# One DMA transpose over 2048 columns in place of two over 1024 in both attentions of a four-layer block

## The chip, the cores and the metric

The kernel runs on one core of a Trainium2 chip. The metric is the device time in microseconds (us) of one execution.
The engines are named as in the profile: PE is TensorE's matmul, PEld its weight load, DVE VectorE, ACT ScalarE, POOL GpSimd, SP SyncE, which here only issues DMAs (SPq is its queue).

## The reference

Four sublayers in turn act on x of 4 batches of 512 tokens by 256 features. Each takes the layernorm of x and adds its result to x:

1. a cross-attention with 16 heads of 64 over 508 keys of a context of 4 x 512 x 192, with low-rank updates of its weights and a second small attention over the last 4 context rows ("A" in the kernel's names);
2. a mixture of 8 experts ("M");
3. a cross-attention with 8 heads of 64 over 512 keys ("C");
4. a gated feed-forward layer with rounded activations and weights ("F").

The attentions are what matters here. For each batch and head:

```
s = jnp.einsum('bhid,bhjd->bhij', q, k) * SCALE
p = jax.nn.softmax(s, axis=-1)
o = jnp.einsum('bhij,bhjd->bhid', p, v)
```

The sum over keys j in the third line needs p with j on the partitions, so p, which is made with queries i on the partitions, has to be transposed.

## The kernel before

One function, `attention`, emits both attentions, C without the low-rank and 4-row parts. Work is cut into G steps. A step n is one block of 128 queries for one pair of heads: 4 batches x 8 pairs x 4 query blocks = 128 steps in A and 4 x 4 x 4 = 64 in C. Half h of a pair is numbered e = 2n + h. A step goes through five engines:

- PE `scores(n)` (L603): six matmuls into two PSUM banks, one for each head; the pair of banks is shared by every second step.
- DVE (L949): one reduction finds both heads' row maxima.
- ACT `weights(n)`: for each head, the exponential twice, once rounded to fp16 into the ring `PHL` (L752, the high part, 8 slots) and once in fp32 into the ring `pr` (L753, 3 slots).
- POOL (L465): for each head, the low part = fp32 minus high part, into the second half of the same slot of `PHL`. It raises `pl_ready` once per head.
- SP (L412): for each head, a DMA transpose of the slot (128 partitions by 1024 columns of fp16: 512 high, 512 low, 256 KB) into half h of `PT[n % 4]`. It waits for `pl_ready` of that head, and on the first head for `pv_done` of step n-4, which frees the buffer.
- PE `weigh(n)` (L621 to L623): 24 matmuls with the transposed blocks as weights. It waits until both transposes of the step have landed (`pt_loaded[n % 4]`).

Each engine's order is written out by hand. PE runs, for g = 0, 1, ...: `scores(g)`, then the jobs that a table plans for g (projections of q and k, transposes of x and of the output, the output projection), then `weigh(g - 3)` (`LAG = 3`). ACT runs `weights(g - 1)` and then copies out the jobs of g. So `scores(n + 4)` stands right behind `weigh(n)` on PE. On SP some plain DMAs stand between the transposes: in A eight loads of the value matrices for the next batch (`load_v`), in both the load of the next batch's context `CT`. `weights(n)` also waits for the transposes of step n-4, which frees its slots of `PHL`.

Of the kernel before, what the change touches and what calls it, by code (L numbers as in the profile page):

```python
# [68 lines left out]
def turn_of(stats, group, nc, name, total):  # L69

    made = stats["turns"].setdefault(group, {})
    if name not in made:
        made[name] = [stats["scope"].enter_context(nc.semaphore(f"{group}_{name}")), 0]
    turn = Turn(made[name][0], made[name][1])
    made[name][1] += total
    return turn
# [58 lines left out]
def attention(nc, tag, X, ident, identb, stats, w, ctx_t, heads, ipa, scratch, x_in=None):  # L135
# [6 lines left out]
    G = B * U  # L142
    KEYS = N - IPA if ipa else N
    HIPA = heads * IPA
    LAG, RING, PRING, PTS, SLOTS, VBANKS = 3, 3, 8, 4, 2, 4
# [37 lines left out]
    with ctx:  # L183
        def sb(name, shape, dt, within=ctx):
            return within.enter_context(nc.sbuf_tensor(f"{tag}_{name}", shape, dt))

        def sem(name, total):
            return turn_of(stats, "attn", nc, name, total)
# [4 lines left out]
        def wait(eng, s, n):  # L193
            eng.wait_ge(s.sem, s.base + n)
# [13 lines left out]
        PHL = sb("PHL", [P, PRING, 2, N], F16)  # L208
        PT = [sb(f"PT{k}", [P, 2, 2 * QT, P], F16) for k in range(PTS)]
# [84 lines left out]
        ws_hi = ipa_sem("ws_hi")  # L294
        ws_split = ipa_sem("ws_split")

        pt_loaded = [sem(f"pt_loaded{k}", 32 * G // PTS) for k in range(PTS)]
        xn_ready = sem("xn_ready", B)
        bias_added = sem("bias_added", B)
        pj_filled = sem("pj_filled", len(jobs))  # L300
# [5 lines left out]
        pl_ready = sem("pl_ready", 2 * G)  # L306
# [18 lines left out]
        def _(sp):  # L325
# [23 lines left out]
            def load_v(b, kt):  # L349
                wait(sp, v_stored[kt], 32 * (B - 1))  # L350
                sp.dma_start(VH[b % 2][:, kt, :, :].rearrange("p h d -> p (h d)"), scratch["vh"][b][:, kt]).then_inc(v_loaded[b % 2].sem, 16)
                sp.dma_start(VL[b % 2][:, kt, :, :].rearrange("p h d -> p (h d)"), scratch["vl"][b][:, kt]).then_inc(v_loaded[b % 2].sem, 16)
# [52 lines left out]
            for n in range(G):  # L405
                b, u = n // U, n % U
                if n >= PTS:
                    wait(sp, pv_done, n - PTS + 1)
                for h in range(2):
                    e = 2 * n + h  # L410
                    wait(sp, pl_ready, e + 1)
                    sp.dma_start_transpose(out=PT[n % PTS][:, h, :, :],  # L412
                                           in_=PHL[:, e % PRING, :, :].rearrange("p s n -> p (s n)")).then_inc(pt_loaded[n % PTS].sem, 16)
                if b + 1 < B:
                    if ipa and 6 <= u < 6 + QT:
                        load_v(b + 1, u - 6)
                    if u == U - 7:
                        if ipa and b == 0:
                            wait(sp, ct_stored[0], 32)
                        wait(sp, pj_filled, JOB["k", b, PAIRS - 1] + 1)  # L420
                        sp.dma_start(CT[:, :, :].bitcast(F32), scratch["ct"][b + 1]).then_inc(ct_loaded[0].sem, 16)
# [53 lines left out]
        def _(pe):  # L475
# [130 lines left out]

            def weigh(n):
                b, c = n // U, n // QT % PAIRS
                wait(pe, pt_loaded[n % PTS], 32 * (n // PTS + 1))
                if n % 2 == 0 and n >= 4:  # L610
                    wait(pe, o_ready, n // 2 - 1)
                if ipa and b and n % U == 0:
                    wait(pe, v_loaded[b % 2], 128 * ((b + 1) // 2))
                vh, vl = VH[b % VBUFS], VL[b % VBUFS]
                for h in range(2):
                    m = (2 * (n % 2) + h) * (DH + 1)
                    o = ps[:, O_BANK + n // 2 % 2, m:m + DH + 1]
                    for kt in range(QT):
                        r = slice(0, P - (N - KEYS) if kt == QT - 1 else P)
                        hi, lo = PT[n % PTS][r, h, kt, :], PT[n % PTS][r, h, QT + kt, :]  # L620
                        mm(o, hi, vh[r, kt, 2 * c + h, :], start=(kt == 0 and h == 0 and n % 2 == 0), stop=False)  # L621
                        mm(o[:, 0:DH], hi, vl[r, kt, 2 * c + h, :], start=False, stop=False)  # L622
                        last = mm(o, lo, vh[r, kt, 2 * c + h, :], start=False, stop=(kt == QT - 1 and h == 1 and n % 2 == 1))  # L623
                last.then_inc(pv_done.sem, 1)
# [51 lines left out]
            for g in range(G + TAIL):  # L676
                if g < G:
                    scores(g)
                for kind, b, k in at.get(g, []):
                    if (kind, b, k) == ("o", 0, 0):  # L680
                        wait(pe, w_split, 4)
                    RUN[kind](b, k)
                if LAG <= g < G + LAG:
                    weigh(g - LAG)

        @block.scalar
        def _(a):
# [55 lines left out]
            def weights(n):  # L743
                wait(a, max_ready, n + 1)
                if n >= PTS:
                    wait(a, pt_loaded[n % PTS], 32 * (n // PTS))
                for h in range(2):
                    e = 2 * n + h
                    o = ps[:, S_BANK + 2 * (n % 2) + h, 0:KEYS]
                    if e >= RING:  # L750
                        wait(a, pl_ready, e - RING + 1)
                    a.activation(PHL[:, e % PRING, 0, 0:KEYS], o, ACT.Exp, bias=nm[:, n % 4, h:h + 1])  # L752
                    a.activation(pr[:, e % RING, 0:KEYS], o, ACT.Exp, bias=nm[:, n % 4, h:h + 1]).then_inc(p_ready.sem, 1)  # L753
# [48 lines left out]
            for g in range(G + TAIL):  # L802
                if 1 <= g <= G:
                    weights(g - 1)
                for u in at.get(g, []):
                    if u[0] in HI_KINDS:
                        high(u)
                if ipa and g < G and g % U == 17:
                    wait(a, ipa_sub, g // U + 1)
                    a.activation(SI[:, 0:QT * heads, :], SI[:, 0:QT * heads, :], ACT.Exp).then_inc(ipa_exp.sem, 1)  # L810
# [957 lines left out]
def network(nc, a, out):  # L1768
    with ExitStack() as ctx:
# [32 lines left out]
        def spare(name, shape, dt):  # L1802
# [6 lines left out]
        }  # L1809
        ctx_t = chunks(a["ctxT"], P)  # L1810
        attention(nc, "A", X, ident, identb, stats, {
            "q": chunks(a["L0_xattn_Wq"], P), "k": chunks(a["wk0"], P), "v": chunks(a["wv0"], P),
            "o": chunks(a["L0_xattn_Wo"], P), "bias": a["bo"], "alpha": a["alpha"], "down": a["down"],
# [6 lines left out]
            "w_out": a["L0_ffn_w_out"].rearrange("e (c p) n -> e p c n", p=P),  # L1820
        })
        attention(nc, "C", X, ident, identb, stats, {
            "q": chunks(a["L1_xattn_Wq"], P), "k": chunks(a["wk1"], P), "v": chunks(a["wv1"], P),
            "o": chunks(a["L1_xattn_Wout"], P), "bias": a["bout"],
# [45 lines left out]
```

## Time and profile before

| | |
|---|---|
| median of 3 runs | 1273.2 us (1271.38 to 1277.29) |
| the profiled execution | 1267.05 us, span 1265.3 us |
| busy share of the span | PE 75%, PEld 58%, DVE 57%, ACT 60%, POOL 52% |
| first attention, steps | about 142 to 592 us of the span |
| third sublayer's attention, steps | about 904 to 1133 us of the span |

The profile is of one execution. Busy shares are over the whole span, with stages of different limits. PE's ends are modelled, since its matmuls are pipelined, so a busy PE isn't PE at its peak. Instructions that issue DMAs do not count as busy, but the trace has their durations. "To landing" counts from the start of an issue to the last update of its semaphore.

### The profile page before, as it was taken

Reading aid. Unit: us, or ns where it says so; the run is one execution under the profiler, and the core shown is the slowest. Engines: PE = TensorE matmul, PEld = TensorE weight load, DVE = VectorE, ACT = ScalarE, POOL = GpSimd, SP = SyncE. Lnnn points to the kernel's source line nnn. Section 1 sums busy time; section 2 is a strip of 40 time slices with the busy share of each in tenths; the row PEclk is TensorE's granted clock in tenths of the full one; section 3 lists DMA queues with packets and bytes.
Section 4 is the critical chain, followed back from the end, with each engine's and each line's share of the span. In section 5 each row is a group of like instructions: output and inputs, shape, how many; then the busy total and the mean of one; then the engine's idle time right before and its main releaser. Section 6 shows DMA issues by size and latency. Waiting matters only on the chain. (4 is left out here: it accounts for less than half of the span.)

```text
span 1265.3 us, 24199 instructions
## 1 busy us (share of the span) xinstructions
PE 954.9 (75%) x9167; PEld 735.3 (58%) x9174; DVE 725.7 (57%) x1301; ACT 757.2 (60%) x1265; POOL 655.7 (52%) x564
## 2 busy tenths in 40 slices
PE   2578778999989999997441999933788888862675
PEld 2456656767666676776330899932556666652343
DVE  3742256765866676573547344437465666538776
ACT  3331387887977788794242444402597787754576
POOL 2420176676776667673257555413186676653121
PEclk9787599999999999997655999976998999976799
DMA  9740299999899899896253222235299998972001
GB/s 251 262 170 5 46 201 166 178 188 198 157 181 203 151 180 171 138 166 111 69 181 98 71 77 77 65 114 190 58 174 172 165 175 151 151 126 100 5 26 39
DMA packets 444193, 171.01 MB, mean 135 GB/s; under 512 B 410128, under 2 KB 427728, under 8 KB 444048
## 3 DMA queue, kind: packets, MB, share of 16 engines
q1 hardware_dynamic: 440336, 159.23, 62.8%
q0 software_dynamic: 3744, 10.23, 2.6%
q8 instruction: 76, 1.25, 0.4%
q14 instruction: 37, 0.30, 0.1%
HBM read 49.68 MB, written 19.05 MB: 54 GB/s over the span
## 5 line engine op out<-in xcount | busy, mean ns | idle before, releaser
L465 POOL TENSOR_TENSOR A_PHL<-A_pr,A_PHL 128x508 f16<-128x508 f32 x256 | 295.2, 1157 | 157.5 <-ACT A_pr L753 157.2
L949 DVE TENSOR_REDUCE A_negmax<-A_ps 128x2 f32<-128x1016 f32 x128 | 155.4, 1214 | 74.3 <-PE A_ps L603 73.7
L465 POOL TENSOR_TENSOR C_PHL<-C_pr,C_PHL 128x512 f16<-128x512 f32 x128 | 148.1, 1163 | 86.5 <-ACT C_pr L753 85.9
L752 ACT ACTIVATE A_PHL<-A_ps,A_negmax 128x508 f16<-128x508 f32 x256 | 179.0, 699 | 21.5 <-DVE A_negmax L949 21.0
L753 ACT ACTIVATE A_pr<-A_ps,A_negmax 128x508 f32<-128x508 f32 x256 | 180.7, 706 | 0.0
L621 PE MATMUL A_ps<-A_VH,A_PT 128*128 128x65 bf16 (+1 forms) x1024 | 110.1, 197 | 34.3 <-DMA A_PT<-A_PHL 33.7
L603 PE MATMUL A_ps<-A_K,A_Q 64*128 64x508 f32 x768 | 125.9, 433 | 11.0 <-ACT A_pr L753 8.9
L621 PEld LDWEIGHTS A_ps<-A_VH,A_PT 128*128 128x128 f16 (+1 forms) x1024 | 93.8, 98 | 64.6 <-DMA A_PT<-A_PHL 52.2
L622 PE MATMUL A_ps<-A_VL,A_PT 128*128 128x64 f16 (+1 forms) x1024 | 109.2, 194 | 0.0
L623 PE MATMUL A_ps<-A_VH,A_PT 128*128 128x65 bf16 (+1 forms) x1024 | 108.9, 195 | 0.0
L949 DVE TENSOR_REDUCE C_negmax<-C_ps 128x2 f32<-128x1024 f32 x64 | 78.2, 1222 | 43.7 <-PE C_ps L603 43.5
L623 PEld LDWEIGHTS A_ps<-A_VH,A_PT 128*128 128x128 f16 (+1 forms) x1024 | 95.8, 98 | 0.0
L622 PEld LDWEIGHTS A_ps<-A_VL,A_PT 128*128 128x128 f16 (+1 forms) x1024 | 95.7, 100 | 0.2
L752 ACT ACTIVATE C_PHL<-C_ps,C_negmax 128x512 f16<-128x512 f32 x128 | 90.3, 706 | 5.1 <-DVE C_negmax L949 4.7
L753 ACT ACTIVATE C_pr<-C_ps,C_negmax 128x512 f32<-128x512 f32 x128 | 91.2, 712 | 0.0
L603 PEld LDWEIGHTS A_ps<-A_K,A_Q 64*128 64x128 f32 x768 | 64.4, 190 | 26.0 <-ACT A_pr L753 10.1
L621 PE MATMUL C_ps<-C_VH,C_PT 128*128 128x65 bf16 x512 | 55.2, 197 | 31.3 <-DMA C_PT<-C_PHL 31.2
L621 PEld LDWEIGHTS C_ps<-C_VH,C_PT 128*128 128x128 f16 x512 | 47.0, 99 | 49.2 <-DMA C_PT<-C_PHL 42.8
L603 PE MATMUL C_ps<-C_K,C_Q 64*128 64x512 f32 x384 | 63.7, 437 | 8.7 <-ACT C_pr L753 6.8
L1431 DVE TENSOR_TENSOR M_XTl<-M_ps,M_XTh 128x512 fp32r<-128x512 f32 x39 | 27.0, 691 | 64.3 <-ACT M_XTh L1314 64.3
L1156 POOL DMA_INDIRECT M_parts<-M_yo,M_dst_u x39 | 38.5, 988 | 45.7 <-DMA M_parts<-M_yo,M_dst_u 41.1
L622 PE MATMUL C_ps<-C_VL,C_PT 128*128 128x64 f16 x512 | 54.7, 195 | 0.0
(353 smaller groups left out, 2750.9 us busy)
## 6 DMA issues: line engine op xcount, KB each, us to landing
A_PT<-A_PHL SPq DMA_TRANSPOSE x256, 3.4
M_rin<-in_L_ffn_w_in SPq DMA_DIRECT2D x8, 512.0 KB, 3.5
M_rout<-in_L_ffn_w_out SPq DMA_DIRECT2D x8, 512.0 KB, 4.0
M_WINh<-M_parts SPq DMA_DIRECT2D x32, 128.0 KB, 2.5
C_CT<-ct_split SPq DMA_DIRECT2D x5, 768.0 KB, 5.1
v_high<-A_VH SPq DMA_DIRECT2D x12, 260.0 KB, 2.7
A_VH<-v_high SPq DMA_DIRECT2D x12, 260.0 KB, 3.1
v_low<-A_VL SPq DMA_DIRECT2D x12, 256.0 KB, 3.4
```

The costliest lines, as they stand in the source:

```text
L465: pool.tensor_tensor(PHL[:, e % PRING, 1, 0:KEYS], pr[:, e % RING, 0:KEYS], PHL[:, e % PRING, 0, 0:KEYS], ALU.subtract).then_inc(pl_ready. ...
L603: last = mm(ps[:, S_BANK + 2 * (n % 2) + h, 0:KEYS], Q[r, c % SLOTS, i, qt * P:(qt + 1) * P], K[r, c % SLOTS, j, 0:KEYS], start=(m == 0), ...
L621: mm(o, hi, vh[r, kt, 2 * c + h, :], start=(kt == 0 and h == 0 and n % 2 == 0), stop=False)
L622: mm(o[:, 0:DH], hi, vl[r, kt, 2 * c + h, :], start=False, stop=False)
L623: last = mm(o, lo, vh[r, kt, 2 * c + h, :], start=False, stop=(kt == QT - 1 and h == 1 and n % 2 == 1))
L752: a.activation(PHL[:, e % PRING, 0, 0:KEYS], o, ACT.Exp, bias=nm[:, n % 4, h:h + 1])
L753: a.activation(pr[:, e % RING, 0:KEYS], o, ACT.Exp, bias=nm[:, n % 4, h:h + 1]).then_inc(p_ready.sem, 1)
L949: v.tensor_reduce(nm[:, g % 4, :], ps[:, S_BANK + 2 * (g % 2):S_BANK + 2 * (g % 2) + 2, 0:KEYS], AX.X, ALU.max, negate=True).then_inc(max_ ...
L1156: pool.indirect_dma_start(out=parts[:, :], out_offset=bass.IndirectOffsetOnAxis(ap=dst_u[:, i:i + 1], axis=0), in_=yo[:, i % RING, :], in_ ...
L1431: v.tensor_tensor(hT[1][:, i % 2, :, :].rearrange("p c n -> p (c n)"), ps[:, HT_BANK + i % 2, :], hT[0][:, i % 2, :, :].bitcast(F32).rearr ...
```

## The change

The two transposes of a step become one. It waits for `pl_ready` of the second head, reads two neighbouring slots of `PHL` (e is even and the ring has 8 slots, so the two are adjacent) as 2048 columns, and writes the whole of `PT[n % 4]`. Its semaphore gets 16 per step instead of 32, and the waits on it count accordingly. Nothing else is changed.

```
-        pt_loaded = [sem(f"pt_loaded{k}", 32 * G // PTS) for k in range(PTS)]
+        pt_loaded = [sem(f"pt_loaded{k}", 16 * G // PTS) for k in range(PTS)]
...
                 if n >= PTS:
                     wait(sp, pv_done, n - PTS + 1)
-                for h in range(2):
-                    e = 2 * n + h
-                    wait(sp, pl_ready, e + 1)
-                    sp.dma_start_transpose(out=PT[n % PTS][:, h, :, :],
-                                           in_=PHL[:, e % PRING, :, :].rearrange("p s n -> p (s n)")).then_inc(pt_loaded[n % PTS].sem, 16)
+                wait(sp, pl_ready, 2 * n + 2)
+                e = 2 * n % PRING
+                sp.dma_start_transpose(out=PT[n % PTS][:, :, :, :].rearrange("p h k n -> p (h k) n"),
+                                       in_=PHL[:, e:e + 2, :, :].rearrange("p r s n -> p (r s n)")).then_inc(pt_loaded[n % PTS].sem, 16)
...
-                wait(pe, pt_loaded[n % PTS], 32 * (n // PTS + 1))
+                wait(pe, pt_loaded[n % PTS], 16 * (n // PTS + 1))
...
-                    wait(a, pt_loaded[n % PTS], 32 * (n // PTS))
+                    wait(a, pt_loaded[n % PTS], 16 * (n // PTS))
```

On SP's queue, in the first batch of A, where the value loads (L351, L352) stand between the transposes, the order is (a row that begins with - is of before, one with + of the change; 128x8x128 is the shape written):

```order
 L351 DMA A_VH<-v_high 128x1040 [waits attn_v_stored0]
 L352 DMA A_VL<-v_low 128x1024
-L412 DMA_TRANSPOSE A_PT<-A_PHL 128x8x128 [waits attn_pl_ready,attn_pv_done]
-L412 DMA_TRANSPOSE A_PT<-A_PHL 128x8x128 [waits attn_pl_ready]
+L411 DMA_TRANSPOSE A_PT<-A_PHL 128x16x128 [waits attn_pl_ready,attn_pv_done]
 L351 DMA A_VH<-v_high 128x1040 [waits attn_v_stored1]
 L352 DMA A_VL<-v_low 128x1024
```

Two issues with a wait each have become one with both waits; the loads keep their places. On PE, early in A, before the change, `scores` of step 6, a projection of k and the beginning of `weigh` of step 3 stand like this (PT3 is the buffer of step 3):

```order
L603 MATMUL A_ps<-A_K,A_Q 128x508 [waits attn_p_ready]
L603 MATMUL A_ps<-A_K,A_Q 128x508 x5
L546 MATMUL A_ps<-A_CT,A_WKh 128x512 [waits attn_pj_free]
L546 MATMUL A_ps<-A_CT,A_WKl 128x512
L546 MATMUL A_ps<-A_CT,A_WKh 128x512 x2
L546 MATMUL A_ps<-A_CT,A_WKl 128x512
L621 MATMUL A_ps<-A_VH0,A_PT3 128x65 [waits attn_pt_loaded3]
L622 MATMUL A_ps<-A_VL0,A_PT3 128x64
L623 MATMUL A_ps<-A_VH0,A_PT3 128x65
```

With the change the same place reads:

```order
L545 MATMUL A_ps<-A_CT,A_WKh 128x512 x2
L545 MATMUL A_ps<-A_CT,A_WKl 128x512
L620 MATMUL A_ps<-A_VH0,A_PT3 128x65 [waits attn_pt_loaded3]
L621 MATMUL A_ps<-A_VL0,A_PT3 128x64
L622 MATMUL A_ps<-A_VH0,A_PT3 128x65
```

Nothing moved on PE but the line numbers, by one.

## Rows read from the trace of the kernel before

**Rows 1.** The page: span, busy time, and clock and DMA in 40 slices.

```profile
span 1265.3 us, 24199 instructions
PE 954.9 (75%) x9167; PEld 735.3 (58%) x9174; DVE 725.7 (57%) x1301; ACT 757.2 (60%) x1265; POOL 655.7 (52%) x564
...
PEclk9787599999999999997655999976998999976799
DMA  9740299999899899896253222235299998972001
```

**Rows 2.** Busy time, granted clock and DMA share of both attentions' steps.

```profile
core 0: us, PE busy (x) PEld busy (x) DVE busy (x) ACT busy (x) POOL busy (x), PEclk, DMA share, GB/s
142.00:592.00 450.00, 402.51 (x4793) 302.26 (x4794) 281.56 (x417) 353.59 (x613) 304.40 (x260) 0.97 0.98 170
904.00:1133.00 229.00, 190.00 (x2301) 140.41 (x2299) 135.44 (x198) 177.54 (x305) 157.32 (x132) 0.95 0.93 159
```

**Rows 3.** The chain of waits: who waited for whom (us, times, longest).

```profile
PEld A_ps L621 <- DMA A_PT<-A_PHL: 52.2, 52, 3.4
PE A_ps L621 <- DMA A_PT<-A_PHL: 33.7, 33, 3.0
PEld C_ps L621 <- DMA C_PT<-C_PHL: 42.8, 33, 4.0
DVE A_negmax L949 <- PE A_ps L603: 73.7, 87, 4.4
ACT A_PHL L752 <- DVE A_negmax L949: 21.0, 18, 3.5
```

**Rows 4.** SP's queue: what its issues waited for, whole span.

```profile
SPq L412 <- POOL A_PHL L465: 107.8, 78, 21.8
SPq L412 <- PE A_ps L623: 35.3, 60, 1.8
SPq L194 <- POOL A_PHL L465: 33.8, 32, 4.4
```

**Rows 5.** The transposes' line: issue min/median/max in ns, and landing.

```profile
L412 SPq DMA_TRANSPOSE A_PT<-A_PHL x256: 1231/1326/3186, 151.3 to 585.8; - x128
L412 SPq DMA_TRANSPOSE C_PT<-C_PHL x128: 1231/1323/3212, 910.8 to 1127.1; - x128
...
DMA to landing us min/median/max: 3.1/3.4/6.8
```

**Rows 6.** The same line from 317.2 to 322.6 us, issues back to back.

```profile
L412 SPq DMA_TRANSPOSE A_PT<-A_PHL x4: 1284/1306/1329, 317.2 to 321.3; - x4
...
DMA to landing us min/median/max: 3.3/3.3/3.3
```

**Rows 7.** The same line from 158.25 to 160.9 us, the queue free before.

```profile
L412 SPq DMA_TRANSPOSE A_PT<-A_PHL x2: 1233/1286/1340, 158.3 to 159.6; - x2
...
DMA to landing us min/median/max: 3.2/3.3/3.4
```

**Rows 8.** That step's second subtraction, L465 from 158.35 to 159.3 us.

```profile
L465 POOL TENSOR_TENSOR A_PHL<-A_pr,A_PHL x1: 1156/1156/1156, 158.3 to 158.3; 128x508 f16<-128x508 f32 x1
```

**Rows 9.** Timeline of the weight loads, the row that waited for that step.

```profile
163.03 0.10 PEld L621 LDWEIGHTS A_ps<-A_VH,A_PT 128*128 128x128 f16 x1 [0.94 <-DMA A_PT<-A_PHL]
```

**Rows 10.** DMA from 158.3 to 162.3 us, in 40 slices of 0.1 us.

```profile
GB/s 0 0 0 0 0 0 0 0 0 0 0 10 131 225 220 212 230 202 205 220 197 207 164 200 162 62 159 225 225 223 195 215 212 205 210 197 182 182 129 90
```

**Rows 11.** DMA from 296 to 304 us, in 40 slices of 0.2 us.

```profile
GB/s 218 281 374 371 308 256 233 214 209 219 189 108 49 18 18 178 293 275 289 289 288 293 225 232 207 207 215 187 125 28 189 215 186 147 152 192 230 230 218 209
DMA packets 5027, 1.67 MB, mean 209 GB/s; under 512 B 4794, under 2 KB 4794, under 8 KB 5026
```

**Rows 12.** POOL's timeline from 317 us: two subtractions a row.

```profile
318.60 2.31 POOL L465 TENSOR_TENSOR A_PHL<-A_pr,A_PHL 128x508 f16<-128x508 f32 x2 [0.30 <-ACT A_pr L753]
321.39 2.31 POOL L465 TENSOR_TENSOR A_PHL<-A_pr,A_PHL 128x508 f16<-128x508 f32 x2 [0.48 <-ACT A_pr L753]
```

**Rows 13.** The page's costliest groups: the exponentials' high parts (L752, with idle before).

```profile
L752 ACT ACTIVATE A_PHL<-A_ps,A_negmax 128x508 f16<-128x508 f32 x256 | 179.0, 699 | 21.5 <-DVE A_negmax L949 21.0
```

**Rows 14.** The transposes' line from 170.15 to 171.6 us, step 6.

```profile
L412 SPq DMA_TRANSPOSE A_PT<-A_PHL x2: 1272/1306/1339, 170.2 to 171.5; - x2
```

**Rows 15.** A plain DMA of 2048 pieces of 1 KB, its issue.

```profile
L364 SPq DMA_DIRECT2D X<-in_x x1: 559/559/559, 7.8 to 7.8; - x1
```

## Prediction
> **What bounds the kernel now.** I read the page first, for where the work lies. The span is 1265.3 us, no engine is busy for more than 75% of it, and the row of DMA digits stands at 9 and 8 through both attentions [rows 1]. Then the busy times of those two stretches: the 128 steps of A take 450 us, 3.52 us each, the 64 of C 229 us, 3.58 us each [rows 2]. That is 679 us of 1265, and the change touches nothing else. In A PE is busy for 402.5 of 450 us, ACT 353.6, POOL 304.4, DVE 281.6, and the granted clock is 0.97, nearly always the upper level of 2.4 GHz. So PE is the fullest engine, without being full.
>
> What PE lacks is in the chain of waits. The weight load at the head of a `weigh` waited for a transpose in 52 of A's 128 steps, 52.2 us together, and in 33 of C's 64, 42.8 us [rows 3]. This is the largest wait of PE in the stretch, and 85 of 192 steps have it. DVE waits for PE's scores 87 times, ACT for DVE's maxima only 18 times: the wait for the transpose is handed round. The path that matters is therefore a ring: `scores(n)`, maxima, exponentials, subtraction, transpose, `weigh(n)`, and right behind that on PE `scores(n + 4)`. Where the transpose of n lands late, PE stops, and step n + 4 starts late.
>
> How late does it land? One transpose holds SP's queue for a median of 1.33 us and lands 3.4 us after its issue began [rows 5]. Two of them per step are 2.65 us of 3.52. In the cheap steps they are back to back: four issues begin from 317.2 to 321.3 us, one every 1.37 us [rows 6], while POOL delivers a pair every 2.8 us [rows 12]. So SP is near its limit there, but only there. Over A, 110 of the 256 issues waited for POOL (78 and 32 times), which says that the queue was free when the data came [rows 4].
>
> **The free queue, before.** The step at 158.3 us shows it. The first head's issue begins at 158.3, as the first subtraction ends; the second at 159.6; each lands 3.2 to 3.4 us after [rows 7]. The second subtraction runs from 158.3 for 1.16 us [rows 8]. So the second head's data is ready 1.16 us after the first's, and its issue begins 1.28 us after: nearly the whole issue of the first head lies under POOL's work on the second. PE goes on at 163.03, after 0.94 us of waiting [rows 9]. From the first subtraction's end that is 4.7 us.
>
> **The free queue, after.** The single issue can't begin until the second subtraction ends, 1.16 us later. How long it then takes is in no row, so I bound it.
> - The DMA's flow by slices of 0.1 us shows nothing for 1.1 us after the issue begins, then some 200 to 230 GB/s, a dip to 62, and again the same for the second head [rows 10]. The transfer of 256 KB thus takes 1.15 to 1.3 us. From its end to the landing there are about 1.0 us left of 3.3.
> - That flow isn't what the DMA engines can do. After a gap at 298.6 us, when two transposes are queued up, it runs at 275 to 293 GB/s for six slices of 0.2 us [rows 11]. So at 215 GB/s the flow is set by the pace at which the issue feeds it, and 512 KB in one instruction take about twice as long, 2.3 to 2.6 us.
> - The landing is then 1.1 + 2.4 + 1.0 = 4.5 us behind the issue's begin (4.4 to 4.7 at the bounds of the transfer). If the engines' best rate held, 512 KB at 290 GB/s, it would be 1.1 + 1.8 + 1.0 = 3.9 us.
>
> From the first subtraction's end: 1.16 + 4.5 = 5.7 us, against 4.7 before. The landing moves back by 1.0 us (0.9 to 1.15; 0.3 by the engines' best rate). What is lost is the overlap of head 0's transfer with head 1's subtraction, which the two issues had.
>
 The flow above agrees with that for 1024 columns; no row shows another size. By it the issue of 2048 columns would be about 2.6 us.
>
> **The busy queue.** Where SP is already behind POOL by t, the first issue before began at t after the first subtraction, and the delay shrinks to 1.0 minus t; behind by 1 us or more it is nothing. One instruction instead of two also saves the gap of 0.04 us and a part of the start: with the dip in rows 10 as its size, 0.1 to 0.3 us of 2.7 per step. That doesn't help much, since POOL's and ACT's pace of 2.8 us per pair is as slow [rows 12]. With an issue of 2.5 us in at least 2.8 the queue will always be waiting for POOL, so each step will pay its landing in full, at the second subtraction's end plus 4.5.
>
> **What else waits.** Behind the issue on SP stand the value loads and the loads of `CT`, wanted a batch later: no cost. `weights(n + 4)` on ACT waits for the same landing, but all its idle time before L752 is put down to DVE's maxima but for 0.5 us of 21.5 [rows 13]. The waits of rows 4 that are put down to PE need a closer look: SP's first issue of a step waits for two semaphores, and `weigh(2)`, begun at 163.03, was over some 6 us before the issue of step 6, which takes its buffer, at 170.2 [rows 9, 14]. So the buffers aren't short, and a delay of 1 us uses a part of that margin. All this is costed at nothing.
>
> **The sum.** A delay on the ring can be paid once in four steps, because the scores of n + 1 to n + 3 are already through PE when `weigh(n)` is held. 192 steps are 48 rounds. If each paid 1.0 us, 48 us. But a step in which PE comes to `weigh` later than the landing absorbs it. 85 of 192 steps were waiting, 44%; I take that share for the rounds as well: 0.44 x 48 x 1.0 = 21 us. It is a choice. Rounds with one waiting step out of four are more than 44%, which raises it; steps where the queue was behind pay less, which lowers it. The first `weigh` of each attention has nothing before it that could cover the delay, 2 x 1.0 us more, and the last ones in part. Together 24 us.
>
> The profiled execution took 1267.05 us, 6 us under the median of the runs, 1273.2. So 1267 + 24 = 1291 in its terms, and 1297 against the median.
>
> **The rivals.**
> 1. *Every round pays.* If PE's slack in the other 107 steps is an effect of the waits themselves (who waited last is late now, so the next isn't), the delays add up fully: 48 x 1.1 = 53, 1326 us. For it: 0.94 to 4 us of waits are spread over both attentions. Against it: in 56% of the steps PE arrived after the landing.
> 2. *It's hidden.* The delay meets queues that were behind anyway and saves 0.1 to 0.3 us of issue per step. If half of all waiting steps were behind by 0.5 us or more, and the issue comes out at 2.2 us (landing 4.2, delay 0.7), the sum is 48 x 0.44 x (0.7 - 0.5) = 4 us: 1277.
> 3. *The issue has a fixed price,* and the kernel is faster. A plain DMA of 2048 pieces took 0.56 us to issue [rows 15], so an issue needn't grow with the pieces. If a transpose of 2048 columns costs 1.3 us of issue and flows at 290 GB/s, it lands 3.9 us behind the second subtraction, and SP's time per step falls from 2.7 to 1.3 us. Free steps then pay 0.3 us, but steps where the queue was behind by a microsecond gain 0.7; over 48 rounds, with 44% on the path and 0.5 us net, -11 us: 1262. It decides from an issue of under about 1.8 us. Against it: the flow of rows 10, slower than the engines can go, starts and ends with each issue. The Trainium skill's "DMA: Bandwidth & Descriptors", section "Rules for kernel authors", has the rule behind this rival, to coalesce many small transfers into a large one; its bound is 64 KB, and each transpose here moves 256 KB, so by the page there is little to win.
>
> **How the numbers follow.** Forecast, between +10 and +40 us: 0.58. Rival 1, over +40: 0.12. Rival 2: 0.17, of which 0.02 falls on the slower side. Rival 3: 0.13. Half a per cent, 6.4 us, is about what a measurement of this kernel can tell from no change. Slower by more than that 0.72, within it 0.15, faster 0.13. The range of 8 in 10 leaves out rival 3 and the top of rival 1: 1269 to 1324. The forecast's own range is 1283 to 1313.
>
> **What would show it.** In the profile after: 192 transposes; an issue of 2.3 to 2.6 us (1.3 would be rival 3) and a landing 4.4 to 4.7 us behind it; nearly all issues waiting for POOL; the weight load at L620 waiting for the transpose in more than half of the steps and for clearly more than 95 us together; step times of 3.65 us or so; the stages M and F unchanged. The prediction is wrong if the issue doesn't grow with the columns, or if PE's waits grow and the attentions' stretches do not, which would say that another engine held the ring.

## The result and the profile after

The change makes the kernel slower: a median of 1303.5 us (1301.2 to 1309.0, 4 runs) against 1272.8 us (1271.4 to 1277.3, 4 runs). The difference of the medians is 30.8 us, a ratio of 1.024. The ratio on record is a little lower, 1.0217 times the time before, with a 95% interval of 1.0172 to 1.0262: slower is clear, more than 2% slower is not.

The page of the changed kernel, span and busy time and the two rows on clock and DMA:

```profile
span 1307.2 us, 24007 instructions
PE 973.5 (74%) x9167; PEld 750.6 (57%) x9174; DVE 731.2 (56%) x1301; ACT 756.1 (58%) x1265; POOL 655.9 (50%) x564
...
PEclk9786699998989999997665899976999899876798
DMA  9640299998999799886153222245298898872001
```

The DMA row is a little lower in both attentions than in [rows 1]. PE, PEld, DVE, ACT and POOL execute as many instructions as before. Where the time went is told by the first and last start of the weighing's weight loads, from the view of the line's tile, for A and for C (the numbers before the semicolon are ns min/median/max, then first and last start in us):

```profile
L620 PEld LDWEIGHTS A_ps<-A_VH,A_PT x1024: 95/97/146, 156.4 to 612.3; 128*128 128x128 f16 x171
...
L620 PEld LDWEIGHTS C_ps<-C_VH,C_PT x512: 95/98/146, 942.3 to 1170.4; 128*128 128x128 f16 x171
```

The kernel before, the same rows:

```profile
L621 PEld LDWEIGHTS A_ps<-A_VH,A_PT x1024: 95/97/137, 156.8 to 590.1; 128*128 128x128 f16 x171
...
L621 PEld LDWEIGHTS C_ps<-C_VH,C_PT x512: 95/98/146, 915.5 to 1132.7; 128*128 128x128 f16 x171
```

A's weighing went from 433.3 to 455.9 us (22.6 more), C's from 217.2 to 228.1 (10.9 more): 33.5 us in the two stretches that the change touches, 0.17 us for each of 192 steps. The two profiled executions lie at opposite ends of the runs: 1308.99 us is the slowest of the four after, 1267.05 us is 4.3 us under the fastest of the four before. The span grew by 41.9 us, and the 8.4 us over the 33.5 lie outside these stretches, where the code is the same; the medians say 30.8.

Not all of the 33.5 us is waiting. The busy times of the two stretches, before and then after (PE's busy time follows the first comma, PEclk is the third figure from the end):

```profile
156.80:590.10 433.30, 390.48 (x4753) 294.92 (x4752) 275.71 (x409) 345.51 (x601) 299.80 (x256) 0.98 1.00 175
915.50:1132.70 217.20, 181.72 (x2264) 135.62 (x2263) 130.97 (x194) 170.09 (x294) 152.69 (x128) 0.95 0.97 164
```

```profile
156.40:612.30 455.90, 397.23 (x4751) 300.84 (x4752) 274.61 (x409) 344.68 (x601) 299.34 (x256) 0.96 0.93 166
942.30:1170.40 228.10, 184.96 (x2262) 138.78 (x2263) 133.08 (x193) 167.79 (x291) 151.88 (x128) 0.93 0.87 156
```

PE took 10.0 us longer for the same instructions, 6.8 in A and 3.2 in C, at a granted clock that fell from 0.98 to 0.96 and from 0.95 to 0.93. The time in which PE was idle grew by 23.5 us. How much of the 10.0 us is due to the change can't be told from one pair of traces: in two executions of one kernel, e3 and e9 below, PE's work in A took 391.9 us at 0.96 and 384.7 us at 0.98.

Now the transposes' line after, to be read beside [rows 5]:

```profile
L411 SPq DMA_TRANSPOSE A_PT<-A_PHL x128: 1317/2059/4549, 151.8 to 606.9; - x128
L411 SPq DMA_TRANSPOSE C_PT<-C_PHL x64: 1317/1992/5076, 937.7 to 1164.0; - x64
...
  PEld A_ps L620: 69.2, 45
  PE A_ps L620: 53.0, 38
  PEld C_ps L620: 49.7, 28
  PE C_ps L620: 39.7, 23
...
DMA to landing us min/median/max: 4.2/4.5/8.1
```

The landing is 4.5 us behind the issue in the median, as the prediction had it, with 3.4 before. The weight loads wait for it 69.2 + 49.7 = 118.9 us, against 95.0 in [rows 3], though in fewer steps, 73 against 85: the waits got longer, not more frequent.

The same step as in [rows 7 to 9] shows the mechanism with a free queue. Its second subtraction on POOL:

```profile
L464 POOL TENSOR_TENSOR A_PHL<-A_pr,A_PHL x1: 1153/1153/1153, 157.7 to 157.7; 128x508 f16<-128x508 f32 x1
```

Its issue on SP and the landing:

```profile
L411 SPq DMA_TRANSPOSE A_PT<-A_PHL x1: 1317/1317/1317, 158.8 to 158.8; - x1
...
DMA to landing us min/median/max: 4.4/4.4/4.4
```

And the weight load that waited for it, from the timeline:

```profile
163.32 0.10 PEld L620 LDWEIGHTS A_ps<-A_VH,A_PT 128*128 128x128 f16 x1 [1.86 <-DMA A_PT<-A_PHL]
```

From the first subtraction's end (157.7, when the second begins) to PE going on it is 5.6 us, against 4.7 before, and PE waited 1.86 us in place of 0.94. The DMA's flow from this issue's begin, in slices of 0.1 us:

```profile
GB/s 0 0 0 0 0 0 0 0 0 0 0 26 146 218 233 215 212 215 195 230 200 215 207 225 223 210 220 223 207 223 223 189 172 136 138 174 244 267 256 238
```

Nothing for 1.1 us, then some 215 GB/s for about two microseconds without the dip of [rows 10]. The issue itself was over after 1.32 us, when less than a tenth of the data had moved.

This step had a free queue; most steps of the kernel before did not. From the start, end and landing times in the traces a round can be followed for every step, from the start of `weigh(n)` to that of `weigh(n + 4)`. The means in us, with e1, the first experiment below, beside them:

| part of the round | A before | A after | A in e1 | C before | C after | C in e1 |
|---|---|---|---|---|---|---|
| `weigh(n)` to the end of the first subtraction of n + 4 | 6.49 | 6.54 | 6.52 | 6.67 | 6.87 | 6.74 |
| from there to the landing | 5.90 | 6.36 | 6.75 | 6.05 | 6.44 | 6.81 |
| from the landing to `weigh(n + 4)` | 1.29 | 1.47 | 1.21 | 1.06 | 1.30 | 1.00 |
| together | 13.68 | 14.37 | 14.48 | 13.79 | 14.60 | 14.55 |

So the landing came 0.46 us later in A and 0.39 in C, not 1.0. In the kernel before, the first issue of a step began more than 0.3 us after its data was ready in 111 of 192 steps, and in the changed kernel in 41: the one issue gives back about half of the delay. The means of a whole round grew by 0.69 and 0.81 us all the same, since PE also came later after the landing.

### The profile page after: what moved, and what is told of

Read it like the earlier page. It is cut to its first block and busy times, and to the rows that moved or that the text cites. A ratio compares the mean times of both kernels' runs of the same rounds, so it can differ in the third digit from the quotient of the medians.

```text
span 1307.2 us, 24007 instructions
## 1 busy us (share of the span) xinstructions
PE 973.5 (74%) x9167; PEld 750.6 (57%) x9174; DVE 731.2 (56%) x1301; ACT 756.1 (58%) x1265; POOL 655.9 (50%) x564
## 5 line engine op out<-in xcount | busy, mean ns | idle before, releaser
L752 ACT ACTIVATE A_pr<-A_ps,A_negmax 128x508 f32<-128x508 f32 x256 | 181.3, 708 | 0.0
L620 PEld LDWEIGHTS A_ps<-A_VH,A_PT 128*128 128x128 f16 (+1 forms) x1024 | 94.6, 99 | 82.8 <-DMA A_PT<-A_PHL 69.2
L602 PE MATMUL A_ps<-A_K,A_Q 64*128 64x508 f32 x768 | 128.7, 442 | 9.2 <-ACT A_pr L752 7.1
L752 ACT ACTIVATE C_pr<-C_ps,C_negmax 128x512 f32<-128x512 f32 x128 | 91.2, 713 | 0.0
L620 PEld LDWEIGHTS C_ps<-C_VH,C_PT 128*128 128x128 f16 x512 | 47.9, 100 | 57.9 <-DMA C_PT<-C_PHL 49.7
L1147 POOL DMA_INDIRECT M_xg<-M_rows,M_src_u x39 | 37.8, 969 | 36.8 <-PE M_ps L1232 34.5
```

Of the source, the lines that this page charges most:

```text
L602: last = mm(ps[:, S_BANK + 2 * (n % 2) + h, 0:KEYS], Q[r, c % SLOTS, i, qt * P:(qt + 1) * P], K[r, c % SLOTS, j, 0:KEYS], start=(m == 0), ...
L1147: pool.indirect_dma_start(out=xg[:, i % AHEAD, :], out_offset=None, in_=rows[:, :], in_offset=bass.IndirectOffsetOnAxis(ap=src_u[:, i:i + ...
```

## The experiments

Each ratio is to the kernel before, run beside it on the same chip: 1278.0 us for e1 to e4, 1277.9 for e5 to e7, 1277.0 for e8 and e9. PTS, the number of `PT` buffers, is 4 throughout.

**e1: two transposes, both behind the second subtraction.** The change's wait without its larger instruction.

```
                 for h in range(2):
                     e = 2 * n + h
-                    wait(sp, pl_ready, e + 1)
+                    wait(sp, pl_ready, 2 * n + 2)
```

> Two transposes of 1024 columns as before, but the first head's also waits for the second head's subtraction. Theory 1 (what costs is the lost overlap of the first head's transfer with the second head's subtraction, on a ring through PE): the second transpose lands 4.7 us behind the second subtraction, 1.1 us later than before, and the kernel takes 1300 to 1310 us, no less than the single transpose does (1303). Theory 2 (the single instruction of 2048 columns is what costs, by its form or size, and its later start matters little): under 1280 us. Issues stay at 1.33 us.

Measured: 1310.7 us, 1.0258 times the kernel before (1.0203 to 1.0313). The waits for transposes:

```profile
PEld A_ps L621 <- DMA A_PT<-A_PHL: 76.2, 56, 3.4
PEld C_ps L621 <- DMA C_PT<-C_PHL: 51.9, 32, 3.9
```

Theory 1 holds. The wait alone, put into the kernel before, costs 32.7 us where the change costs 30.8; no loss is left for the larger instruction. It lands 0.4 us sooner than the second of two issues does (the table above), but e1's rounds are only 0.11 us longer for it in A and no longer in C, and the intervals of the two ratios overlap: a gain from it isn't shown.

**e2: four transposes of 512 columns.** The high part of each head goes as soon as ACT is done with it, the low part behind POOL (the first one of all behind POOL too, because of the columns that POOL clears). The semaphore counts, not shown, go to 64 a step.

```
-                    wait(sp, pl_ready, e + 1)
-                    sp.dma_start_transpose(out=PT[n % PTS][:, h, :, :],
-                                           in_=PHL[:, e % PRING, :, :].rearrange("p s n -> p (s n)"))...
+                    for s, ready in enumerate((p_ready, pl_ready)):
+                        wait(sp, pl_ready if e == 0 else ready, e + 1)
+                        sp.dma_start_transpose(out=PT[n % PTS][:, h, s * QT:(s + 1) * QT, :],
+                                               in_=PHL[:, e % PRING, s, :])...
```

> Four transposes of 512 columns in a step; the two high parts wait for ACT alone, the two low parts for POOL. Theory 1: the last one carries only 128 KB behind the second subtraction and lands 1.1 + 0.6 + 1.0 = 2.7 us after it in place of 3.5, so the kernel gets 0.8 x 21 = 17 us faster than before, 1255 us, provided that an issue of 512 columns costs some 0.65 us. If an issue has a fixed part of 0.3 us or more, four of them take over 3.6 us of SP in a step and the queue bounds the attentions: 1300 us or more. Theory 2: larger instructions are worse, so this is the best of the three: also faster, but the landing would not follow the size.

Measured: 1684.1 us, 1.316 times (1.309 to 1.323). The transposes' line, and the DMA's flow from 500 to 504 us in slices of 0.1 us:

```profile
L413 SPq DMA_TRANSPOSE A_PT<-A_PHL x512: 1188/1265/2713, 149.4 to 863.2; - x171
L413 SPq DMA_TRANSPOSE C_PT<-C_PHL x256: 1194/1265/2399, 1195.0 to 1545.0; - x128
...
DMA to landing us min/median/max: 2.4/2.5/6.3
```

```profile
GB/s 103 19 0 0 0 0 0 90 223 205 233 220 207 110 24 0 0 0 0 0 77 202 223 218 225 210 126 32 0 0 0 0 0 54 207 212 236 215 205 146
```

The issue of 512 columns takes 1.27 us, as good as that of 1024 (1.33). The flow shows it: 0.6 us of data at the same 215 GB/s, and then half a microsecond of nothing until the next issue's data comes. Four issues are 5.1 us of SP in a step, and A's issues are 714 us apart from first to last, 5.6 us a step. The landing does come sooner, 2.5 us behind its issue, but the queue bounds everything. So halving what an issue carries, from 256 to 128 KB, saves next to nothing of its 1.3 us. At their shortest the issues of 512, 1024 and 2048 columns take 1.19, 1.23 and 1.32 us; of 2048 columns only 13 of 192 stayed under 1.4 us, and the medians are 2.06 and 1.99. The second branch of the expectation came true, and far more strongly than a fixed part of 0.3 us would have it.

**e3 and e4: PE weighs a step later.** Two transposes and one, with the ring over PE a step longer.

```
-    LAG, RING, PRING, PTS, SLOTS, VBANKS = 3, 3, 8, 4, 2, 4
+    LAG, RING, PRING, PTS, SLOTS, VBANKS = 4, 3, 8, 4, 2, 4
```

> The kernel before with LAG = 4, so that PE weighs a step later and has one step (about 3.5 us) more until it needs the transposed blocks. Theory 1: the waits of the weight loads for transposes (52 and 43 us before) fall below a third, and what remains is bound by PE's own work and by ACT: 1240 to 1260 us. Theory 2 says nothing of this kernel but that it is not slower than before by much. Rival: another engine holds the ring too, the waits only move to it, and the time stays within 1265 to 1280.

> The changed kernel (one transpose of 2048 columns) with LAG = 4. Theory 1: the later landing by 1 us is absorbed by the longer ring, so this takes the same as the two transposes with LAG = 4, within 8 us. Theory 2: it stays 20 us or more above them, since the larger instruction's cost is in the queue and not in PE's slack.

Measured: 1243.3 us with two (0.9721 times before, 0.9658 to 0.9784), 1242.3 us with one (0.9703, 0.9647 to 0.9759). Both beat both kernels, and the expectations hold. The waits of the weight loads, with two and then with one transpose:

```profile
PEld A_ps L621 <- DMA A_PT<-A_PHL: 13.2, 8, 3.1
PEld C_ps L621 <- DMA C_PT<-C_PHL: 13.0, 9, 2.8
```

```profile
PEld A_ps L620 <- DMA A_PT<-A_PHL: 17.2, 13, 3.3
PEld C_ps L620 <- DMA C_PT<-C_PHL: 13.4, 14, 2.8
```

With one the landing is as late as ever, 4.7 us behind its issue in the median against 3.4 with two; the 31 us between the two forms are gone. So the later landing costs only where PE has to wait for it, and no price of the larger instruction shows elsewhere.

**e5 and e6: PE weighs a step sooner.** The same two kernels with `LAG = 2`, to see how a delay adds up.

> Two transposes as before, LAG = 2: PE needs each step's blocks one step earlier, the ring closes every three steps. Theory 1: nearly every weighing waits, a round is about 1.0 (scores) + 1.2 + 2.8 + 1.2 + 3.5 (landing behind the subtraction) + 0.9 us = 10.6 us and more for three steps; the attentions get some 50 to 130 us longer, 1330 to 1400 us.

> One transpose of 2048 columns, LAG = 2. Theory 1 with the rule that a later landing is paid once in each round of the ring: 192 steps are 64 rounds of three, nearly all of them waiting, so this kernel takes 50 to 65 us more than the two transposes with LAG = 2. Rival: each step pays by itself, 192 x 1.0, over 150 us more; or the delay is hidden again in other waits, under 30 us more.

Measured: 1414.3 us with two (1.1093, 1.1033 to 1.1152), 1468.2 us with one (1.1473, 1.1414 to 1.1532). The difference is 53.8 us. The waits, two and one:

```profile
PEld A_ps L621 <- DMA A_PT<-A_PHL: 130.2, 77, 5.1
PEld C_ps L621 <- DMA C_PT<-C_PHL: 79.9, 44, 4.6
```

```profile
PEld A_ps L620 <- DMA A_PT<-A_PHL: 150.8, 79, 4.3
PEld C_ps L620 <- DMA C_PT<-C_PHL: 92.7, 46, 4.2
```

The two transposes took longer than the 1330 to 1400 us that I had expected, but the difference between the two kernels is in its range. There are 64 rounds of three steps, so 53.8 us are 0.84 us a round. Taken from the traces as in the table above, the mean landing behind the first subtraction's end came 0.81 us later in A and 0.73 in C, and the round 0.91 and 0.71: with nearly every round waiting, the rule of rounds holds. Neither rival comes near. PE's same work took 22.9 us longer here, at 0.89 and 0.87 of the clock against 0.91 and 0.89; the traces don't show how much of that lies on the ring.

**e7: one transpose in C alone.**

```
+    PER = 32 if ipa else 16
...
+                if not ipa:
+                    wait(sp, pl_ready, 2 * n + 2)
...
+                else:
+                    for h in range(2):
```

> One transpose in the third sublayer's attention alone, two in the first. By the rule of rounds the third's 64 steps are a third of the change, and its steps waited more often (33 of 64 against 52 of 128): 10 to 13 us over before, and the first attention's stretch keeps its 450 us. Rival: the loss sits in one of the two attentions alone, then this is either within 3 us of before or 25 us over it.

Measured: 1288.9 us against 1277.9, 1.0092 times (1.0058 to 1.0127), 11 us more, as expected. In its trace the weight loads wait for transposes in C alone as in the changed kernel, 50.0 us in 28 steps, and in A as before, 53.5 us in 49. C's stretch from the first weighing to the last is 226.5 us, against 217.2 before and 228.1 after. A's is 437.6 against 433.3 with the same code, so that a single trace's stretch is good to some 4 us. C carries a part of the loss that fits its share of the steps, and the rest is left for A.

**e8 and e9: LAG = 5, beside LAG = 4 again,** both with two transposes.

> Two transposes, LAG = 5. With LAG = 4 the weight loads still waited 13 us in each attention for transposes. Theory 1: the ring has one step more, these waits go and at most some 10 us are gained, 1233 to 1243 us, if the four buffers PT suffice; but the transpose of a step now waits for a weighing only one step before it, so a rival is that the buffers hold SP's queue and it is slower than with LAG = 4, 1250 us or more.

> The two transposes with LAG = 4 once more, beside LAG = 5 on the same chip: 1238 to 1248 us.

Measured: 1266.7 us with `LAG = 5` (0.9895, 0.9860 to 0.9930), 1239.8 us with `LAG = 4` (0.9690, 0.9643 to 0.9736). The expected gain of some 10 us didn't come: 5 is 27 us slower than 4. With 5 the waits for transposes are nearly gone, 7.1 and 8.5 us against 19.6 and 12.2. In their place PE's weight load for the transposes of the output (L573) waits for the division by the softmax's sums (DVE, L899). With `LAG = 5`, and then 4:

```profile
PEld A_ps L573 <- DVE A_O L899: 14.7, 7, 2.4
PEld C_ps L573 <- DVE C_O L899: 5.5, 3, 2.3
```

```profile
PEld A_ps L573 <- DVE A_O L899: 0.9, 1, 0.9
PEld C_ps L573 <- DVE C_O L899: 0.9, 1, 0.9
```

These transposes are planned for a fixed step, 21 behind the start of a half, and the last weighing of the half stands on PE at step 15 + `LAG`: with 5 that is the step just before, and the division hasn't had its time. It is 18.4 us of PE's waits. My rival named another cause, SP held by the buffers, and its premise is in the trace: in 47 steps the first issue began within 0.3 us of the weighing that frees its buffer. But it doesn't reach PE, which comes to `weigh` more than 5 us after the landing in the mean. That a table planned a step later would gain the time back was not tried.

## Why the prediction was right, and where it wasn't

The prediction said 1297 us and slower; it is 1303.5. The mechanism was right. That the number came so near is in part luck: in the sum 0.44 x 48 x 1.0 the share was too low by about half and the delay too high by about two. By its steps:

- **The lost overlap**: right. Head 0's issue and transfer used to lie under POOL's subtraction for head 1. e1 puts that wait alone into the kernel before and gets the whole loss.
- **The landing with a free queue**, 4.5 us behind the issue and 1.0 later from the first subtraction: right, 0.9 later in the step shown.
- **The busy queue**: right in kind, then left out of the sum, though in 111 of 192 steps the issue before was over 0.3 us behind its data. Over all steps the landing came only 0.46 us later in A and 0.39 in C; over the steps in which PE waited, 0.5 us.
- **The share of rounds that pay**: 0.44 was the choice of the sum, taken from steps. Of four steps in a row at least one waited in 0.85 of the cases in the trace before, 41 of 48 rounds. The prediction had named this itself (one waiting step in four is enough), but gave it no weight. With the two figures as measured the sum is 0.85 x 48 x 0.5 = 20 us, near the 21 predicted.
- **What is left**: the two stretches grew by 33.5 us, not 20. By the same reckoning e1 comes to 33 of its 36.1 us (a delay of 0.8), and the pair with `LAG = 2` to 50 of 52.3, so the gap is the changed kernel's own. In its rounds PE comes 0.18 and 0.24 us later after the landing, some 10 us in all, and PE's same work took 10.0 us longer at a lower granted clock, for which the prediction had no term. Whether the one is the other no run here decides.
- **The issue's length**, 2.3 to 2.6 us in proportion to the columns: wrong. At its shortest it is 1.32 us, in the median 2.06 and 1.99. I read the pace of the flow as the pace of the issue. They are two things: e2 shows that an issue costs 1.27 us even for half the columns, and in the step shown the flow goes on for two microseconds when the issue is over. Why the median is longer than the minimum isn't settled.
- **The prediction's own sign of error**, an issue that doesn't grow with the columns: it came at the shortest issues (1.23 to 1.32 us) and not in the median. It was ill chosen. What PE waits for is the landing, and that grew from 3.4 to 4.5 us.
- **Rival 1**, that every round pays, was near the truth on the rounds and had the delay, 1.1 us, twice too large; 53 us were its price. **Rival 2** was right that the delay often meets a queue that was behind anyway, but the loss is not 4 us. **Rival 3** had a part of its premise right, an issue that doesn't double, and its result wrong: SP's time was freed, but what PE waits for is the landing, and that follows the data's readiness and the flow. It took 290 GB/s for the flow, a rate that only queued transposes had reached.
- **"Waiting in more than half of the steps"**: wrong, 73 of 192. **"Nearly all issues waiting for POOL"**: 141 of 192. **"Clearly more than 95 us together"**: right, 118.9. **Step times of 3.65 us**: from 142 us to the end of the last weighing A took about 472 us, 3.69 a step, by the measure that gave 3.52 before, and C 3.75.

## What to carry to other kernels

Before two transfers are merged, ask what the first one was hiding under. If its data is ready sooner than the second's and the queue is free, merging delays the whole by the gap between the two, plus the transfer of the first's data, less the price of one issue: here 1.16 + 1.1 - 1.28 = 1.0 us. Where the queue was already behind, the delay is smaller. Saved issue time is worth something only where the queue is what others wait for: going from two issues a step to one gained nothing that the runs show, and four made the queue the limit of the kernel. When an engine waits for a late landing in a software pipeline, look first at the distance between producer and consumer. One more step of lag gained 35 us, and the two forms of the DMA then took the same time; a step too many ran into a table planned for the old distance.

## What the runs showed of the hardware

A DMA transpose of fp16 within SBUF, 128 partitions, held SP's queue for 1.27 us at 512 columns, 1.33 at 1024 and some 2.0 at 2048 in the median, and for 1.19, 1.23 and 1.32 us at the shortest. It landed 2.5, 3.4 and 4.5 us after its issue began in the median. The first data moved 1.1 us after the issue began, and the flow was some 215 GB/s at each size while one transpose's data moved alone. I had not expected that the issue's price isn't in proportion to the size, since in the kernel before issue and flow are as long as each other and look like one thing.

PE's granted clock was lower the more PE stood idle, and the same instructions then took longer: in A, from the first weighing to the last, 390.5 us of PE's time in 433.3 us at 0.98 in the kernel before, 425.4 in 530.6 at 0.91 with two transposes and `LAG = 2`, 494.7 in 711.0 at 0.80 in e2. How much of a wait's price in a round is owed to this was not separated.
